# Attention scores and values regrouped: four heads per key block in one step, row score matmuls ahead of column score matmuls within each pair

## What is computed

```python
x = x + attn_b(_layernorm(x), Wqkv, bqkv, Wout, bout)

qkv = (x @ Wqkv + bqkv).reshape(B, L, 3, n_heads, head_dim)      # B 8, L 1024, 16 heads of 16
q, k, v = (qkv[:, :, 0], qkv[:, :, 1], qkv[:, :, 2])
scores = jnp.einsum('bqhd,bkhd->bhqk', q, k) / math.sqrt(head_dim)
bias = -jnp.abs(pos[None, :] - pos[:, None]).astype(jnp.float32)
scores = scores + slopes[None, :, None, None] * bias[None, None]
probs = jax.nn.softmax(scores, axis=-1)
out = jnp.einsum('bhqk,bkhd->bqhd', probs, v).reshape(B, L, D)
return out @ Wout + bout
```

## Time and profile before

| what | value |
|---|---|
| median of the runs | 3313.69 us |
| span of the profiled execution | 3314.4 us |
| PE busy | 3139.1 us, 95% of the span |
| VectorE (DVE) busy | 2521.7 us, 76% |
| ScalarE (ACT) busy | 1985.8 us, 60% |
| row maxima reduction L1896 | 2048 instructions, 685 ns each |
| exponential L1814 | 1024 instructions, 1026 ns each |
| row scores L1639, column scores L1701 | 2048 matmuls each, 480 and 469 ns each |
| values L1655 | 8192 records, 385 ns each |
| bias blocks L1560 | 4096 matmuls, 197 ns each |

### The profile page before, as it was taken

How to read it: one execution, slowest core, us unless ns; L and a number is a source line. 1 busy time by engine, 2 the same in 40 slices (tenths; PEclk the granted TensorE clock), 3 DMA queues, 4 the chain that set the end, 5 groups by cost and what they waited for, 6 DMA issues and landing times. The chain is left out here.

```text
span 3314.4 us, 79004 instructions
## 1 busy us (share of the span) xinstructions
PE 3139.1 (95%) x31780; PEld 1960.7 (59%) x31780; DVE 2521.7 (76%) x4848; ACT 1985.8 (60%) x2967; POOL 780.8 (24%) x916
## 2 busy tenths in 40 slices
PE   7999999995999689999999999999999999998999
PEld 3666666663888555555555555555555555546888
DVE  6777777755888478778878788788787887837887
ACT  2544555432666317776767676767676766775665
POOL 3445454532222201111110110111111101002222
PEclk8999999986999759999999999999999999998999
DMA  1000000003111422122222131222221312202111
GB/s 54 15 15 27 27 28 27 21 15 105 52 52 51 100 39 46 25 49 47 46 50 46 25 71 25 46 50 46 50 43 27 66 30 42 42 12 95 52 58 39
DMA packets 110349, 145.51 MB, mean 44 GB/s; under 512 B 21792, under 2 KB 94256, under 8 KB 109200
## 3 DMA queue, kind: packets, MB, share of 16 engines
q1 hardware_dynamic: 108776, 136.78, 17.5%
q0 software_dynamic: 768, 2.77, 0.4%
q10 hardware_dynamic: 440, 0.90, 0.2%
HBM read 53.79 MB, written 38.24 MB: 28 GB/s over the span
## 5 line engine op out<-in xcount | busy, mean ns | idle before, releaser
L1896 DVE TENSOR_REDUCE b_half_max<-banks 128x1 f32<-128x512 f32 x2048 | 1304.3, 685 | 290.5 <-PE banks L1560 174.9
L1814 ACT ACTIVATE b_p_t<-banks 128x1024 f32<-128x1024 f32 x1024 | 1040.3, 1026 | 372.1 <-PE banks L1560 231.2
L1639 PE MATMUL banks<-b_k_stack,b_q_stack 62*128 62x512 f32 x2048 | 835.0, 480 | 26.4 <-issue 10.4
L1701 PE MATMUL banks<-b_q_stack,b_k_stack 64*128 64x512 f32 x2048 | 832.9, 469 | 8.8 <-ACT b_p_t L1814 7.7
L1655 PE MATMUL banks<-b_p_t,b_v 128*17 128x256 f32 x8192 | 628.4, 385 | 0.2 <-ACT b_p_t L1814 0.2
L1701 PEld LDWEIGHTS banks<-b_q_stack,b_k_stack 64*128 64x128 f32 x2048 | 344.4, 185 | 373.0 <-issue 322.8
L1639 PEld LDWEIGHTS banks<-b_k_stack,b_q_stack 62*128 62x128 f32 x2048 | 342.0, 188 | 75.5 <-DVE b_half_max L1896 33.9
L1560 PE MATMUL banks<-b_unit,b_tables 64*128 64x64 bf16 x4096 | 373.1, 197 | 0.0
L1137 ACT ACTIVATE ffn_relu<-banks,ffn_scale_fc 128x512 f32<-128x512 f32 x256 | 176.2, 688 | 205.3 <-PE banks L1069 205.3
L1082 PE MATMUL banks<-ffn_proj_t,ffn_r_hi 128*128 128x256 f32 x1024 | 262.2, 289 | 2.7 <-DVE ffn_r_lo L1263 2.5
L1560 PEld LDWEIGHTS banks<-b_unit,b_tables 64*128 64x128 bf16 x4096 | 186.2, 96 | 120.7 <-issue 70.6
(11 more groups left out here) (247 smaller groups left out, 4937.7 us busy)
## 6 DMA issues: line engine op xcount, KB each, us to landing
ffn_x<-x SPq DMA_DIRECT2D x32, 512.0 KB, 3.8
b_q_stack<-b_qk_hi SPq DMA_DIRECT2D x252, 64.0 KB
b_k_stack<-b_qk_hi SPq DMA_DIRECT2D x252, 64.0 KB
a_x<-hidden_states SPq DMA_DIRECT2D x16, 512.0 KB, 4.1
x<-a_x SPq DMA_DIRECT2D x16, 512.0 KB, 2.9
x<-ffn_x SPq DMA_DIRECT2D x16, 512.0 KB, 2.8
b_x<-x SPq DMA_DIRECT2D x8, 1024.0 KB, 5.5
out<-ffn_x SPq DMA_DIRECT2D x16, 512.0 KB, 2.9
```

What stands on the lines that cost most here:

```text
L1639: last = pe.matmul(m, q_stack[rows, slot, qb * P:(qb + 1) * P], k_stack[rows, slot, half * BANK:(half + 1) * BANK], start=True, stop=not h ...
L1701: last = pe.matmul(out, k_stack[stack, slot, kb * P:(kb + 1) * P], q_stack[stack, slot, half * BANK:(half + 1) * BANK], start=True, stop=n ...
L1814: act.activation(p_t[use % P_BUFS][:, :, :], scores[use % 2], ACT.Exp, scale=slopes()[pair][0]).then_inc(p_made, 1)
L1896: dve.tensor_reduce(half_max[:, (pair + rg * PAIRS) * QB + qb, half:half + 1], misc.at["max", g, turn], axis=AX.X, op=ALU.max, negate=True ...
```

## The change

A step of `attend` becomes a key block with all four heads. Within a pair both row matmuls are issued first, with their bias blocks, then both column matmuls with theirs; the bias blocks of the two heads alternate. The values of one whole key block (both parts) follow after both pairs. `LEAD` goes from 16 to 20 and `TURN` from 2 to 4, and the other generators are merged between key blocks, not between heads. The other engines get the same order. The number and shapes of the instructions stay. The core of the diff:

```diff
-        LEAD, TURN = 16, 2
+        LEAD, TURN = 20, 4
+        BLOCKS = HALVES * QB
...
-            def follow(t, pair):
-                if pair == 0:
-                    if (t - 2) % QB == 0:
-                        values_of(t - 2, 0)
-                        values_of(t - 2, 1)
-                        step()
-                    else:
-                        values_of(t - 2, 1)
-                elif (t - 1) % QB:
-                    values_of(t - 1, 0)
-                    step()
+            def follow(t):
+                step()
+                if (t - 1) % QB:
+                    if (t - 2) % QB == 0:
+                        values_of_both(t - 2)
+                    values_of_both(t - 1)
...
 def find_maxima():
                         last = pe.matmul(m, q_stack[...], k_stack[...], start=True, stop=not here, ...)
-                        if not here:
+                        if here:
+                            outs.append((rg, m[:, at:at + P]))
+                        else:
                             last.then_inc(row_scores, 1)
+                    yield
+                    if turn % ROWGROUPS == ROWGROUPS - 1:
+                        if outs:
+                            add_block_bias(outs, g, pair, int(qb >= CT), row_scores)
+                            outs = []
                         yield
-                        if here:
-                            add_block_bias(m[:, at:at + P], g, pair, rg, int(qb >= CT)).then_inc(row_scores, 1)
                         yield
...
+                for t, half, kb in key_blocks(g):
+                    here, at = kb // CT == half, kb % CT * P
+                    for pair in range(PAIRS):
+                        use, outs = PAIRS * t + pair, []
+                        for rg in range(ROWGROUPS):
+                            next(rows, None)
+                        next(rows, None)
+                        if use >= 2:
+                            pe.wait_ge(p_made, use - 1)
+                        for rg in range(ROWGROUPS):
+                            ...
+                            last = pe.matmul(out, k_stack[...], q_stack[...], start=True, stop=not here, ...)
+                            ...
+                        if here:
+                            add_block_bias(outs, g, pair, int(kb < CT), col_scores)
+                        next(rows, None)
+                    follow(t)
                     yield
```

More of the change, by code:

```diff
@@ L1483, in row_turns, with key_blocks @@
                 yield g, turn, pair, qb, half, 1 - turn % 2
-        def turns(g):
+        def key_blocks(g):
             for half in range(HALVES):
                 for kb in range(QB):
-                    for pair in range(PAIRS):
-                        for rg in range(ROWGROUPS):
-                            yield (g * HALVES + half) * QB + kb, half, kb, pair, rg
+                    yield (g * HALVES + half) * QB + kb, half, kb
         def tails(weigh, conclude):
@@ L1554, in tensor, with add_block_bias @@
         def tensor(pe):
-            def add_block_bias(out, g, pair, rg, variant):
-                rows = slice(rg * STACK, (rg + 1) * STACK)
+            def add_block_bias(outs, g, pair, variant, ready):
                 for part in range(PARTS):
                     cols = slice(part * STACK, (part + 1) * STACK)
-                    last = pe.matmul(out[:, cols], tables[rows, g % GROUPS * PAIRS + pair, 1 - variant, part, :], unit[rows, :],
-                                     start=False, stop=part == PARTS - 1, tile_position=(rg * STACK, 0))
-                return last
+                    for rg, out in outs:
+                        rows = slice(rg * STACK, (rg + 1) * STACK)
+                        last = pe.matmul(out[:, cols], tables[rows, g % GROUPS * PAIRS + pair, 1 - variant, part, :], unit[rows, :],
+                                         start=False, stop=part == PARTS - 1, tile_position=(rg * STACK, 0))
+                        if part == PARTS - 1:
+                            last.then_inc(ready, 1)
             def normalize(b):
@@ L1694, in attend @@
                 pe.wait_ge(v_made, QB * (b + 1))
[L1695 to L1710, removed]
+                for t, half, kb in key_blocks(g):
[8 more added lines that the diff above has]
+                        for rg in range(ROWGROUPS):
+                            first, slot = place(g, pair + rg * PAIRS)
+                            stack, out = slice(first, first + STACK), scores[use % 2][:, rg, :]
+                            last = pe.matmul(out, k_stack[stack, slot, kb * P:(kb + 1) * P], q_stack[stack, slot, half * BANK:(half + 1) * BANK],
+                                             start=True, stop=not here, tile_position=(first, 0))
+                            if here:
+                                outs.append((rg, out[:, at:at + P]))
+                            else:
+                                last.then_inc(col_scores, 1)
+                        if here:
+                            add_block_bias(outs, g, pair, int(kb < CT), col_scores)
+                        next(rows, None)
+                    follow(t)
                     yield
@@ L1805, in attend @@
             def attend(g, rows):
-                for t, half, kb, pair, rg in turns(g):
-                    if rg == ROWGROUPS - 1:
-                        use = 2 * t + pair
+                for t, half, kb in key_blocks(g):
+                    for pair in range(PAIRS):
+                        use = PAIRS * t + pair
                         act.wait_ge(col_scores, ROWGROUPS * (use + 1))
@@ L1814, in attend @@
                         act.activation(p_t[use % P_BUFS][:, :, :], scores[use % 2], ACT.Exp, scale=slopes()[pair][0]).then_inc(p_made, 1)
-                    next(rows, None)
-                    if rg == ROWGROUPS - 1:
-                        follow(t, pair)
+                        for rg in range(ROWGROUPS):
+                            next(rows, None)
+                    follow(t)
                     yield
@@ L1932, in attend @@
             def attend(g, rows):
[L1933 to L1936, removed]
+                for t, half, kb in key_blocks(g):
+                    for _ in range(GROUP):
+                        next(rows, None)
+                    follow(t)
                     yield
```

18 lines of the change are left out of this document (10 added, 8 removed).

## The result

The changed kernel takes 3577.68 us, the median of four runs (3572.75 to 3588.61), against 3314.74 for the kernel before in the same comparison. The ratio is 1.079, with a 95% interval from 1.076 to 1.081: 7.9% slower. The forecast was 3528, the range 3405 to 3610. The profiled execution's span grew from 3314.4 to 3571.2 us, by 257 us where 215 were forecast.

A forecast was written before the change was run, and what follows sets the result against it. The prediction took PE as the bound, busy 392.4 of 400 us in the attention. Its terms, 188 - 27 + 34 + 10 + 10 + 5 - 5 = 215 us on 3314.4, gave 3529 (median 3528.7), range 3405 to 3610.

The forecast's parts named there:

- The pace now, and the savings: PE in the attention: a key block costs 2.72 us; values in one go and bias blocks together would save 87 us.
- The ring's wait: Three-bank ring: a block's fourth row matmul waits for the first one's reduction; block 3.09 us for 2.72, 188 us more.
- smaller terms: Effects outside the steady block, such as divisions, projections, transposes and the lead; together between -10 and +60 us.
- a and d: First and fourth of a key block's four row score matmuls (b, c between); mean distance forecast at 1.315 us.
- a free bank: Rival: the bank wait doesn't bind, so only the savings are left; 3200 us, chance 0.08.
- half the loss: Rival: the second pair of a key block streams without any gap; 3410 us, chance 0.12.
- a tie: Rival: gain and wait cancel, within 7 us of the old time; chance 0.02.
- divisions: VectorE's two divisions after a finished half's transposes hold the next reduction by 0.53 us, 64 times: 34 us more.
- projections and transposes: Row matmuls waiting after q and k projections, 10 us more, and after the next batch's transposes, 10 us more.
- turned maxima's wait: The wait at the maxima's transposes, claimed to stay as before, with nothing added.
- The lead: Start of the maxima, where rows run alone: the third row matmul's bias blocks wait behind the fourth; 5 us more.
- The clock: Rival: new pauses lower the clock for a tenth of the blocks, 92 us on top, 3620 us; chance 0.08.

The follow-up runs named there:

- e3: The changed kernel with the maxima taken over every second column only, so each reduction reads 256 elements in place of 512: 3408.6 us, ratio 1.026.
- e1: The changed kernel with the values of a key block again cut in two parts, one behind each pair: 3370.9 us, ratio 1.014.
- e4: The changed kernel with the column matmuls ahead of the row matmuls within each pair: 3517.1 us, ratio 1.060.
- e8: The changed kernel with values in two parts and the column matmuls ahead of the row matmuls in each pair: 3308.5 us, ratio 0.9955.
- e6: The kernel before with only LEAD 20 and TURN 4: 3326.0 us, ratio 1.002.
- e5: The changed kernel plus four thrown-away column score matmuls in the pause before a block's fourth row score matmul: 3604.4 us, ratio 1.085.

## Why the prediction was right, and where it was short

**The pace now, and the savings.** The price of pairs and parts held: both parts in one go cost 0.99 us in the changed kernel too.

**The ring's wait.** The distances read from the double pairs, 1.28 and 1.35 us, are what the changed kernel shows: the median over all blocks is 1.36, 58% of them lie between 1.25 and 1.40 and none below. In most of the others more time passes, because other work is merged in. A block was to take 3.09 us; undisturbed ones take 3.00 to 3.17. The quiet group grew by 6.0 us, 0.375 a block where 0.37 was forecast; some of the smaller terms are in that figure, so the closeness is in part luck. e3 shows the cause by shortening the reduction alone, e1 by putting half of the values between a and d. The three rivals with a free bank, half the loss or a tie fell.

**The smaller terms.** The stage grew by 246 us. Of these about 37 belong to the clock (below), and 209 remain, against 210 for the forecast's terms inside the stage (188 - 27 + 34 + 10 + 10 - 5). That match is luck: the single terms were off in both directions. The divisions were to delay the next reduction by 0.53 us. The timeline of VectorE behind the transposes:

```profile
2455.85 0.25 DVE L1923 RECIPROCAL b_recip<-banks 128x16 f32<-128x16 f32 x1
2456.13 0.42 DVE L1925 TENSOR_TENSOR b_att<-banks,b_recip 128x256 f32<-128x256 f32 x1
2456.47 2.61 DVE L1906 TENSOR_REDUCE b_half_max<-banks 128x1 f32<-128x512 f32 x4
```

The reduction of the a that starts at 2455.51 begins at 2456.47, 0.96 us after it where 0.54 to 0.61 is usual, so 0.35 to 0.4 late at this place. The wait for the other users of the ring was undersized in turn: e4 and e8 put the rows' place ahead of the columns at 61 us, clock included, where the prediction had 20 us for projections and transposes and took the turned maxima's wait to stay as it was. (By the comparison of blocks below, the clock may make up 25 of the 61, which leaves some 36 for the waits.) It didn't stay. The changed kernel around such a place:

```profile
1796.34 0.30 PE L1629 MATMUL banks<-b_ident,b_row_max 128*64 128x128 f32 x1
1796.57 0.50 PE L1638 MATMUL banks<-b_k_stack,b_q_stack 62*128 62x512 f32 x2
...
1798.85 0.50 PE L1638 MATMUL banks<-b_k_stack,b_q_stack 62*128 62x512 f32 x2 [1.30 <-ACT b_shift_full L1783]
```

c is the third take after the transpose, and ScalarE makes the copy only after an exponential. PE stands still for 1.30 us, where the longest wait of this kind was 0.6.

**The lead** cost 11.5 us (the first column matmul comes at 1243.7 for 1232.2), and 5 were forecast; e6 puts 2.1 of them down to LEAD and TURN.

**The clock.** This was a rival with a chance of 0.08, and the prediction let it stand for itself instead of adding a part of it. In the stage the clock was at its lower level for 102 us, against 7 before. Windows of the changed kernel, behind the place just shown:

```profile
1800.00:1810.00 10.00, 9.76 (x108) 4.92 (x97) 7.20 (x13) 5.82 (x6) 0.00 (x0) 0.84 0.03 7
1810.00:1820.00 10.00, 8.82 (x86) 4.69 (x84) 9.34 (x27) 6.84 (x8) 2.25 (x4) 1.00 0.01 2
1820.00:1830.00 10.00, 9.91 (x89) 4.96 (x89) 5.55 (x10) 4.28 (x5) 2.23 (x3) 0.66 0.01 2
```

The clock column reads 0.84 and 0.66, so part of these stretches ran at 1.2 GHz. In the stage there are 15 such dips once it is warm, and each begins just behind a wait of 0.68 to 1.30 us for the turned maxima, a projection or the next batch's transposes; most waits of that size have no dip behind them. PE looks busier there (9.76 and 9.91 of 10), because its matmuls take longer. Each key block that met a dip can be set against the same place of the other batches: 39 us more in all, against 2 before. That is an estimate from one execution; the same comparison gives 13 us in e4.

The 257 us of the two spans are then 37 for the clock, 11.5 for the lead and 209 for all the waits together; this last figure is what remains and not a measurement of its own.

The step that failed is thus the clock's price, which the sum put at nothing: about 37 us, most of the 42 by which the span outgrew the forecast. The argument was that steady pauses leave the clock at 1.00 and that nothing else would lower it. The longer waits at a few places per batch had not been looked at. Nor are the steady pauses without effect: e5 fills only those and leaves the long ones (its row matmuls still wait for the turned maxima 25 times, up to 1.3 us), and the time at the lower clock halves. So the dips begin behind long waits, and how many come depends on the short pauses as well. Of the rule cited from the Trainium skill (TensorE: Matmul & The Clock Gate, "A second HAM failure mode: psum-queue depth-cycling"), the trace agrees with the mechanism and not with its extent: the clock went up and down, but for about a twentieth of the stage.

**What stays open.** e5 halved the time at the lower clock without making the kernel faster, so no run separates the clock's price from the waits. It rests on comparisons of blocks: for the half that e5 removed, they give 18 us place by place and 12 by the sums above. Why only some of the long waits bring a dip is not shown. The gain of 0.45% in e8 was not taken apart into the bias blocks' order and the merging by key blocks.

## What to carry to other kernels

Before matmuls that share a ring of PSUM banks are moved together, measure the distance from one of them to the next user of the same bank and compare it with the reader's latency: here 1.28 to 1.35 us for a reduction of 0.69, and an order that put less than that between them lost 0.3 to 0.5 us in every undisturbed key block, though no engine was full. A large piece of work that needs no bank from the ring, here the values, is worth more between two bursts of such matmuls than saved by 0.13 us at their end. Every other user of the ring counts as well, with all that is queued ahead of its reader, and in a burst the matmuls that need the ring should stand last.

## What the runs showed of the hardware that was not expected

A falling clock hides in the busy share, in the midst of the attention as in the lead: in windows of 10 us PE was busy for 9.91 at a mean granted clock of 0.66 and for 8.82 at 1.00, so a busy share near 1 says nothing about the clock. A filled pause in turn can keep the clock up and still not pay: four matmuls more per block left undisturbed blocks at 3.0 to 3.2 us and halved the time at the lower clock, and the kernel still took 27 us longer.
